# Taking the filler products out of the passes of a four-layer cross-attention kernel

## What is computed

```python
x = L0(x, ctx)   # 16-head causal attention, norm 1; 16-head cross attention, norm 2;
                 # relu(x @ w1 + b1) @ w2, norm 3
x = L1(x, ctx)   # 16-head attention of width 8 with a row mask
x = L2(x, ctx)   # linear attention: one encoder layer on ctx, one decoder layer on x
x = L3(x, ctx)   # 8-head attention, then a scan over time: s = silu(s @ A.T) + u_t
```

## Time and profile before

| | before |
|---|---|
| median of the runs | 2123.61 us |
| profiled execution | 2124.64 us |
| its span, first to last instruction | 2122.9 us |
| PE busy | 1872.6 us (88%), 13625 matmuls |
| DVE busy | 1339.7 us (63%) |
| ACT busy | 1109.4 us (52%) |
| POOL busy | 239.0 us (11%) |
| mean granted TensorE clock | 0.978 of full |

### The profile page before, as it was taken

The page is one execution under the profiler, slowest core; times in us unless marked ns, Lnnn a source line. Parts: engine busy times, 40 slices in busy tenths (PEclk is TensorE's granted clock), DMA queues, the critical chain, the costliest instruction groups (busy, mean ns, idle before and its releaser), DMA issues.

```text
span 2122.9 us, 36204 instructions
## 1 busy us (share of the span) xinstructions
PE 1872.6 (88%) x13625; PEld 1198.0 (56%) x13625; DVE 1339.7 (63%) x3612; ACT 1109.4 (52%) x3858; POOL 239.0 (11%) x263
## 2 busy tenths in 40 slices
PE   5887998899988998899988998899988998877699
PEld 2555565646655565546655565556655566544345
DVE  3554768577775768577775768577775768554410
ACT  3452845557363845557363845567473836433222
POOL 0001011010212011010212011010202011010000
PEclk9999999999999999999999999999999999988999
DMA  6000000000000000000000000000000000000001
GB/s 196 1 1 6 12 1 1 1 17 2 1 1 6 12 2 1 1 17 1 1 1 6 13 1 1 1 17 2 1 2 6 1 1 1 1 1 1 1 16 25
DMA packets 25138, 20.14 MB, mean 9 GB/s; under 512 B 2243, under 2 KB 22790, under 8 KB 24966
## 3 DMA queue, kind: packets, MB, share of 16 engines
q1 hardware_dynamic: 24966, 17.83, 2.9%
HBM read 15.73 MB, written 2.10 MB: 8 GB/s over the span
## 4 chain that ended last, share of the span: by engine, by line
PE 54%; DVE 23%; ACT 17%; issue 4%; POOL 2%; SPq 1%; DMA 0%; POOLq 0%; DVEq 0%; ACTq 0%
PE ps L825 12%; PE ps L833 11%; ACT probs L1474 7%; PE ps L873 5%; ACT s_probs L1474 4%; PE ps L974 3%; PE ps L897 3%; DVE neg_max L1735 3%; DVE tok L1755 3%; DVE stats L1742 3%; PE ps L883 2%; PE ps L998 2%; PE ps L1422 2%; PE ps L869 2%; PE ps L821 2%
## 5 line engine op out<-in xcount | busy, mean ns | idle before, releaser
L1474 ACT ACTIVATE probs<-ps,neg_max 128x128 f32<-128x128 f32 x1024 | 362.2, 395 | 147.7 <-DVE neg_max L1735 146.5
L1474 ACT ACTIVATION_READ_ACCUMULATOR probs<-ps,neg_max 128x1 f32 x1024 | 238.8, 234 | 0.0
L1474 ACT ACTIVATE s_probs<-ps,s_max 128x128 f32<-128x128 f32 x672 | 183.7, 396 | 95.6 <-DVE s_max L1735 95.6
L1735 DVE TENSOR_REDUCE neg_max<-ps 128x4 f32<-128x512 f32 x256 | 164.5, 684 | 89.8 <-PE ps L873 89.8
L647 POOL TENSOR_TENSOR rstd<-var_eps,minus_half 128x4 f32<-128x4 f32 x88 | 94.4, 1072 | 1068.0 <-DVE var_eps L1748 1067.2
L1742 DVE BATCH_NORM_STATS2 stats<-ps 128x6 f32<-128x128 f32 x352 | 78.2, 284 | 181.4 <-PE ps L833 179.6
L1777 DVE TENSOR_TENSOR probs<-probs,inv 128x512 f32<-128x512 f32 x256 | 177.1, 692 | 8.8
L1468 ACT ACTIVATE probsT<-ps 128x512 f32<-128x512 f32 (+1 forms) x270 | 164.2, 629 | 27.3 <-PE ps L883 13.6
L883 PE MATMUL ps<-ident,probs 128*128 128x128 f32 x1024 | 156.5, 281 | 8.6 <-ACT queries L1468 4.6
L873 PEld LDWEIGHTS ps<-keys,queries 64*128 64x128 f32 x2048 | 125.7, 189 | 54.7 <-issue 54.7
L873 PE MATMUL ps<-keys,queries 64*128 64x128 f32 x2048 | 150.5, 287 | 0.0
(11 more groups left out here) (296 smaller groups left out, 3421.8 us busy)
## 6 DMA issues: line engine op xcount, KB each, us to landing
x_in<-in_x SPq DMA_DIRECT2D x8, 256.0 KB, 3.0
c_in<-in_ctx SPq DMA_DIRECT2D x8, 256.0 KB, 3.2
skip_in<-in_mask_BxS_ik SPq DMA_DIRECT2D x8, 256.0 KB, 3.1
out<-headsT SPq DMA_DIRECT2D x28, 64.0 KB, 1.8
valid_in<-in_mask_BxS_bf SPq DMA_DIRECT2D x8, 64.0 KB, 3.7
w_qkv_sa<-in_L_xattn_sa_wq SPq DMA_DIRECT2D x1, 512.0 KB
w_qkv_sa<-in_L_xattn_sa_wk SPq DMA_DIRECT2D x1, 512.0 KB
w_qkv_sa<-in_L_xattn_sa_wv SPq DMA_DIRECT2D x1, 512.0 KB
```

The costliest lines, as they stand in the source:

```text
L1474: last = A(dst[:, u % dst.shape[1], h * 128:h * 128 + 128], bank(st, (tag, "s", u))[:, h * 128:h * 128 + 128], ACT.Exp, bias=src_max[:, u ...
L1735: V.tensor_reduce(dst[:, u % 2, :], bank(st, (tag, "s", u)).rearrange("p (h k) -> p h k", h=4), AX.X, ALU.max, negate=True).then_inc(max_r ...
```

## The change

All three entries of `BUSY` become 0, so that `keep_busy` issues nothing there. The 22 products of each pass (8, 8 and 6), 176 in all, are gone. Waits, banks, orders and all other instructions stay as they are, also the fillers of the last stage and of the scan.

```diff
-BUSY = {"ln2": 16, "ln3": 16, "end": 12}
+BUSY = {"ln2": 0, "ln3": 0, "end": 0}
```

## The result

The changed kernel takes 2143.53 us (median of 4 runs, 2141.47 to 2146.20) against 2122.12 us (2118.90 to 2124.22) before: a ratio of 1.0103, 95% interval 1.0084 to 1.0122. The profiled execution took 2141.47 us, with a span of 2139.6 us.

What follows compares the result with a forecast made beforehand. PE's order and clock were taken to set the pace. Losses of 6.6 us (second norm) and 13.6 us (third norm and end), 20.2 us on the profiled 2124.64, gave 2144.8, less 1.0 to the median: 2143.8 us, range 2129 to 2157.

Steps and rivals of the forecast that it cites:

- The step on which all rests: Without fillers PE's gaps at second and third norm bring clock falls, in six of passes 1 to 7 and all eight.
- Second norm: Falls on the turned blocks and feed-forward products behind the second norm: six passes at 1.1 us, 6.6 us lost.
- third rival: At both norms falls last longer, as thin work doesn't bring the clock back: +35 us at most, 2151 to 2159 us; chance 0.08.
- Third norm and end: A 6.82 us fall from about 440.8 slows turned blocks and products: eight passes at 1.7 us, 13.6 us (6.4 to 19).
- Gain of the fillers' going: Earlier turning of `x_in` at the pass's end without fillers: between 0 and 1.1 us, taken as 0.
- DVE's chain is nearer to the next wait: At the pass's end, the reason for taking 0 of the possible 1.1 us: the next product waits for DVE's hand-over anyway.
- Tail of the cross attention: Existing falls behind a 2.04 us idle stretch, in six of seven passes, priced at most 0.97, on average 0.64 us.
- The clock stays up: Gaps left in passes 1 to 7 are harmless, only pass 0's third norm falls anew: about 2125 us; chance 0.08.
- Cheap falls: Falls at 14 places at 0.64 us each: +9 us, 2133 us; at the cheapest price +2 us; chance 0.13.
- Longer falls: Falls at both norms outlast the time taken, the second seeing 6.8 us too: +35 us at most, 2151 to 2159 us; chance 0.08.
- The kernel gets faster: Shifted timing removes the five existing falls (3.2 us) and end fillers give 1.1 us: 2119 us; chance 0.03.

Runs made afterwards that it cites:

- the two runs with a tail filler and all of `BUSY`: Kernel before plus 7 products at the cross attention's tail: at the wrong step 2130.50 us (1.0034), one step earlier, in the 2.04 us gap, 2118.95 us (0.9982).
- The transpose fillers: Kernel before with each filler product at the norms and pass's end replaced by two float32 identity blocks turned in transpose mode: 2125.67 us, ratio 1.0003.
- the tail filler: Kernel before, all its fillers kept, plus 7 products in PE's 2.04 us gap at the tail of the cross attention: 2118.95 us, ratio 0.9982.

## Why the prediction was right

**The clock.** The step on which all rests, that the clock falls at both norms once the fillers are gone, held everywhere: in the profiled execution the clock fell at the second norm in seven passes of seven (six were taken) and behind the third in eight of eight. (In pass 0 the fall at the third norm is not only the change's doing: the traces of the two runs with a tail filler and all of `BUSY` show one there too.) The transpose fillers show that it is PE's work in the gaps that matters.

**Second norm.** Taken 6 x 1.1 = 6.6 us. Measured 9.8 us behind the first feed-forward product in seven passes (1.43 us on average in passes 1 to 6) and 1.1 us ahead of it, on the turned blocks, in three of them: 10.9 us. The term was too small for three reasons: the seventh fall; two falls that lasted for 6.83 us and cost 2.3 us each (1.8 us on the feed-forward products, 0.5 us on the turned blocks), just as the third rival had it; and the others, of 3.41 us, which cost 0.97 to 1.50 us, mean 1.27, against the 1.1 us taken.

**Third norm and end.** Taken 8 x 1.7 = 13.6 us. Measured 1.2 us in pass 0, 1.42 us on average in passes 1 to 6 and 0.4 us up to the hand-over of pass 7: 10.1 us. In pass 1 the clock did not fall at about 440.8 us, as I had put it, but at 443.57 us, behind the turned blocks of `main_normed`, which ran at full speed (0.63 us). So the slow stretch lay wholly on the products and cost what I had named for that case (2.4 us): from 443.48 to 449.98 PE needed 6.50 us before and 9.05 us for the same part after, 2.55 us lost. But more was given back. The spare time that I put ahead of 449.98 (0.4 us) is small beside the one behind it, PE's wait of 0.98 us for the masks, which I had not looked at. The two terms, missed by 4.3 us one way and 3.5 us the other, mostly cancel in the sum of 20.2 us. That the forecast of 2143.8 us meets 2143.5 us this closely is luck: the mechanism was right, its prices only roughly. Two side readings were off as well: slow products add about 36 us to PE's busy time, not some 20, and PE waits 1.94 and 2.67 us for `main_normed`, not 2.1 and 2.9.

**Gain of the fillers' going.** I took 0 out of 0 to 1.1 us. Where no clock falls, a pass without the end's fillers is 0.25 to 0.3 us shorter, about 2 us in all, above the upper bound. The step that failed is "DVE's chain is nearer to the next wait": `x_in` feeds ACT, which empties it, and then GpSimd. Without the end's fillers both start 0.17 us earlier in the pass, GpSimd's products overlap the first mask less (0.74 us in place of 0.91), and PE goes on from the masks 0.17 us earlier, while the start of `x_side` has not moved at all. The rest of the gain comes in small steps over the pass. In the changed kernel it is buried.

**Tail of the cross attention.** That its falls (0.54 us on average over the six passes of rows 6) would stay was nearly right: 0.41 us after, in all six. That they are the clock's doing was argued ahead of the result and is shown by the tail filler.

**Rivals.** "The clock stays up" is out: it fell behind idle stretches of 1.94 and 2.67 us. "Cheap falls" (+9 us) is out by the interval. "Longer falls" is out as the rule, but two of the seven at the second norm were of its kind. "The kernel gets faster" is out; but the way it named, to be rid of the tail's falls, is real and gave 0.9982.

**What stays open.** The falls about 104 us into a pass stand in seven of the fourteen traces, in one to five passes each, with and without the end's fillers; they cost 1.6 us each. No run was made on them. Nor was the last stage looked into.

## What to carry to other kernels

Judge a filler by two rows: the idle time that it stands in, and the granted clock over the dense work that follows. In a gap, ahead of a fall, it is free and saves about 1.4 us here; in no gap it costs its length; behind a fall it took 1.6 times its length here. As a fall either comes at a place or does not, half the fillers can be enough, and a second gap that nobody filled may be worth more than trimming the first. And when a stretch runs slow, look for what comes back at the next wait of the same engine before you sum the loss.

## What the runs showed of the hardware

Float32 blocks turned on TensorE (16 in 1.91 us) kept the granted clock at 2.4 GHz as well as bf16 products did (8 in 1.89 us): no fall at either norm in passes 1 to 6, and a ratio of 1.0003 against 1.0103 without either.

DVE's 128x512 bf16 instruction with two operands took 1.38 us beside GpSimd's float32 work and 0.43 us without it, and the one-operand mask 0.73 to 0.91 against 0.42 us. The Trainium skill (SBUF — State Buffer, Who interferes with whom) says that a VectorE instruction with two operands in SBUF contends with a GpSimd instruction that reads SBUF, for a pair of ports that they share. The traces agree: `mask_sa` went from 1.37 to 0.43 us when `x_bias` was moved and GpSimd's `qT` no longer ran beside it, and `qT` itself from 1.46 to 1.27 us. Why the mask with one operand is longer beside GpSimd, no run shows.
